# A selective scan whose output is projected in tiles of 16 steps by 8 samples instead of 128 steps of one sample

## What is computed

```python
def step(h, inputs):
    ad, bd, xt, ct = inputs
    h = jnp.clip(h * ad[:, :, None] + bd[:, :, None] * xt[:, None, :], -10.0, 10.0)
    yt = jnp.einsum('bd,bdh->bh', ct, h)
    return (h, yt)
...
y = ys.transpose(1, 0, 2) + D * xn
return y * jax.nn.silu(gate) @ W_out.T
```

## Time and profile before

| | us |
|---|---|
| median of 3 runs | 709.54 (709.09 to 712.57) |
| the profiled execution, its time | 711.52 |
| the same, its span (first to last instruction) | 709.7 |
| DVE busy | 500.8 (71%) |
| PE busy | 508.3 (72%) |
| ACT, POOL busy | 263.4, 130.1 |
| DMA | 64.88 MB, mean 91 GB/s |

### The profile page before, as it was taken

How to read it: one execution, slowest core, us unless ns; L and a number is a source line. 1 busy time by engine, 2 the same in 40 slices (tenths; PEclk the granted TensorE clock), 3 DMA queues, 4 the chain that set the end, 5 groups by cost and what they waited for, 6 DMA issues and landing times.

```text
span 709.7 us, 10868 instructions
## 1 busy us (share of the span) xinstructions
PE 508.3 (72%) x3248; PEld 301.2 (42%) x3264; DVE 500.8 (71%) x820; ACT 263.4 (37%) x513; POOL 130.1 (18%) x136
## 2 busy tenths in 40 slices
PE   3567888788888887999993000077777767898878
PEld 3455556465654644678883000011111112233367
DVE  2724759577585766556666898289999967999942
ACT  2314554535545342267663547011222212222211
POOL 5302012020210200060000235203131102223100
PEclk9858999999999998999996555579999989999999
DMA  9734161724427150021000134645545545556441
GB/s 356 229 67 100 36 118 21 132 44 89 96 38 133 31 102 0 1 115 63 0 0 1 49 116 157 105 77 103 98 95 99 106 86 106 132 124 143 85 149 52
DMA packets 44889, 64.88 MB, mean 91 GB/s; under 512 B 19536, under 2 KB 34256, under 8 KB 41152
## 3 DMA queue, kind: packets, MB, share of 16 engines
q1 hardware_dynamic: 41520, 59.26, 37.6%
q0 software_dynamic: 784, 3.15, 1.1%
q10 hardware_dynamic: 2560, 2.16, 0.9%
HBM read 41.88 MB, written 22.61 MB: 91 GB/s over the span
## 4 chain that ended last, share of the span: by engine, by line
PE 31%; DVE 23%; issue 21%; DMA 9%; ACT 7%; POOL 6%; SPq 2%; ACTq 0%; POOLq 0%; DVEq 0%
DVE zst L1377 19%; PE bank L718 6%; ACT ex L540 5%; PE bank L736 4%; DMA bst<-bd_d 3%; DMA qst<-mT 3%; PE bank L746 3%; PE bank L773 2%; PE bank L975 2%; PE bank L1061 2%; PE bank L965 2%; PE bank L727 2%; PE bank L756 2%; DVE mx L1175 2%; POOL xpart L416 2%
## 5 line engine op out<-in xcount | busy, mean ns | idle before, releaser
L1377 DVE CUSTOM_DVE_ANT_0 zst<-zst,bank,hi 128x512 f32<-128x512 f32 x256 | 191.5, 748 | 34.7 <-PE bank L965 26.1
L965 PE MATMUL bank<-xst,bst 128*128 128x512 bf16 x240 | 83.1, 399 | 98.6 <-DMA bst<-bd_d 60.2
L648 ACT ACTIVATE yb<-bank,ybias 128x512 f32<-128x512 f32 x64 | 44.0, 688 | 178.3 <-PE bank L975 157.9
L965 PEld LDWEIGHTS bank<-xst,bst 128*128 128x128 bf16 x256 | 24.6, 98 | 179.0 <-DVE zst L1377 109.4
L1175 DVE TENSOR_REDUCE mx<-bank 128x2 f32<-128x512 f32 x128 | 80.0, 686 | 18.2 <-PE bank L736 17.1
L540 ACT ACTIVATE ex<-bank 128x512 f32<-128x512 f32 x128 | 66.0, 608 | 41.2 <-PE bank L746 23.6
L975 PE MATMUL bank<-zst,cst 128*32 128x512 f32 x512 | 69.7, 617 | 0.7 <-DVE zst L1377 0.7
L1193 DVE TENSOR_TENSOR esum<-ex 128x1024 f32<-128x1024 f32 x32 | 39.1, 1223 | 43.0 <-ACT ex L540 43.0
L1237 DVE SCALAR_TENSOR_TENSOR acc<-xrp,wcv,acc 128x256 f32<-128x256 f32 x96 | 40.2, 481 | 29.3 <-ACT acc L580 28.7
L877 PE MATMUL bank<-xres,win 128*128 (+1 forms) x256 | 57.6, 382 | 1.2 <-ACT gateT L585 0.7
L389 POOL TENSOR_TENSOR qk<-qk,part 128x512 f32<-128x512 f32 x16 | 20.1, 1258 | 196.6 <-ACT part L502 196.6
(11 more groups left out here) (169 smaller groups left out, 712.9 us busy)
## 6 DMA issues: line engine op xcount, KB each, us to landing
qk_d<-part SPq DMA_DIRECT2D x64, 96.0 KB, 2.5
xs_d<-xpart SPq DMA_DIRECT2D x16, 384.0 KB, 2.6
xst<-xs_d SPq DMA_DIRECT2D x32, 192.0 KB
xst<-xs_d SPq DMA_DIRECT2D x32, 128.0 KB
y_d<-yb SPq DMA_DIRECT2D x128, 32.0 KB
ytk<-y_d SPq DMA_DIRECT2D x16, 256.0 KB, 3.7
bst<-bd_d SPq DMA_DIRECT2D x32, 102.0 KB
qst<-qk_d SPq DMA_DIRECT2D x8, 384.0 KB, 4.7
```

Source lines behind the costliest of these rows:

```text
L648: nc.scalar.activation(yb[:, par, g, :], bank[4 + n % 2][:, :], ACT.Identity, bias=ybias[:, bass.ds(i * (2 * CH // 4) + n, 1)]).then_inc(s ...
L965: mm(bank[k][:, :], bst[:, par, step, :], xst[:, par, step, :], start=True, stop=True)\
L1377: v._custom_dve(bass.dve_ops.TENSOR_ADD_SAT, out=zst[:, t % ZR, :], in0=zst[:, (t - 1) % ZR, :], in1=bank[t % 4][:, :], s0=hi[:, t:t + 1], ...
```

## The change

Rounds stay 16 steps (`RS`). What differs:

- An output tile is one round: 16 steps x 8 samples. The read-outs of all 16 steps accumulate in one bank (4 or 5 in turn): the weights of a step are laid in `cst` with shifted windows so that step 4g+k writes partitions 32k + 8g to 32k + 8g + 7, and zero elsewhere. `y_d` and the 128 + 16 DMAs of it are gone.
- ACT takes the bank with the bias to `ytk`, POOL adds D*xn from `dxk`, PE transposes, ACT copies and also makes the strided copy `x1s` (two instructions of 128 columns), POOL gates in four instructions of 128 columns, PE projects, ACT copies to `ob` (two buffers), SP stores with four DMAs. Tile r is done in round r+1, fifteen of them inside the scan; the last has DVE for the add and the gate.
- D*xn: POOL scales ten tiles before the first round and two in each of rounds 1 to 3. SP stores each to `dx_d` (eight DMAs of 256 KB before the loop, eight in round 3) and loads each round's 256 KB in `dxk` with four DMAs, two buffers.
- The scan inputs lie in two buffers of 16 steps instead of 8. The first round is loaded in halves (x: 8, 8, then 16 steps; b the same). A b load is two DMAs, rows 0 to 47 and 48 to 50.
- SP, POOL, ACT and PE have their rounds written out instead of loops.
- `ybias` comes from 16 small products instead of 4; POOL clears larger buffers at 301 us.

```diff
-            def load_x(par, ch):
+            def load_x(slot, first, count, name):
                 at = 0
                 for run in (3, 2, 1):
-                    sp.dma_start(xst[at:at + run * B, par, :, :],
-                                 xs_d[0:run, :, bass.ds(ch * CH, CH), :].rearrange("k b t c -> (k b) t c"))\
-                      .then_inc(s[f"ld_x{par}"], 16)
+                    sp.dma_start(xst[at:at + run * B, slot, first % RS:first % RS + count, :],
+                                 xs_d[0:run, :, first:first + count, :].rearrange("k b t c -> (k b) t c"))\
+                      .then_inc(s[name], 16)
                     at += run * B
-            def load_b(par, ch):
-                sp.dma_start(bst[0:KU, par, :, :], bd_v[:, bass.ds(ch * CH, CH), :]).then_inc(s[f"ld_b{par}"], 16)
+            def load_b(slot, first, count, name):
+                for lo, hi in ((0, KX), (KX, KU)):
+                    sp.dma_start(bst[lo:hi, slot, first % RS:first % RS + count, :],
+                                 bd_v[lo:hi, first:first + count, :]).then_inc(s[name], 16)
...
-            def store_chunk(par, ch):
-                for k in range(4):
-                    sp.dma_start(y_d[bass.ds(ch * CH, CH), :, :].rearrange("(g k) b c -> k b g c", k=4)[k],
-                                 yb[32 * k:32 * k + B, par, :, :]).then_inc(s[f"yst{par}"], 16)
+            def store_dx(half):
+                for b in range(B):
+                    sp.wait_ge(s["dx_ready"], half * B + b + 1)
+                    sp.dma_start(dx_d[half * P:(half + 1) * P, b, :], xc[:, b * HALVES + half, :]).then_inc(s[f"dx_out{half}"], 16)
+            def load_dx(r):
+                if r % (R // 2) == 0:
+                    sp.wait_ge(s[f"dx_out{r // (R // 2)}"], 16 * B)
+                if r >= 2:
+                    sp.wait_ge(s["ysum_ready"], r - 1)
+                for k in range(4):
+                    sp.dma_start(dxk[32 * k:32 * k + 32, r % 2, :], dx_by_tile[r, k])\
+                      .then_inc(s[f"ld_dx{r % 2}"], 16)
+            def store_out(r):
+                sp.wait_ge(s["ob_ready"], r + 1)
+                for k in range(4):
+                    sp.dma_start(out_by_tile[r, k], ob[32 * k:32 * k + 32, r % 2, :])\
+                      .then_inc(s[f"o_out{r % 2}"], 16)
...
-            load_x(0, 0)
-            load_x(1, 1)
+            load_x(0, 0, RS // 2, "ld_xf")
+            load_x(0, RS // 2, RS // 2, "ld_x0")
+            load_x(1, RS, RS, "ld_x1")
             sp.wait_ge(s["bd_out0"], 16 * (len(PAIRS) + 3))
-            load_b(0, 0)
-            load_b(1, 1)
+            load_b(0, 0, RS // 2, "ld_bf")
+            load_b(0, RS // 2, RS // 2, "ld_b0")
+            load_b(1, RS, RS, "ld_b1")
             store_b(1)
             sp.wait_ge(s["bd_out1"], 16 * (len(PAIRS) + 3))
+            store_dx(0)
+            sp.wait_ge(s["yb_done"], 1)
+            load_dx(0)
+            load_dx(1)
+            for i in range(R):
+                if i + 2 < R:
+                    sp.wait_ge(s["u_done"], (i + 1) * RS)
+                    load_x(i % 2, (i + 2) * RS, RS, f"ld_x{i % 2}")
+                    load_b(i % 2, (i + 2) * RS, RS, f"ld_b{i % 2}")
+                if i == 3:
+                    store_dx(1)
+                if i >= 1 and i + 1 < R:
+                    load_dx(i + 1)
+                if i >= 2:
+                    store_out(i - 2)
...
+            # POOL
+            fill_c(0)
+            fill_c(1)
             pool.wait_ge(s["rem0"], NT)
             pool.wait_ge(s["sq_done"], NT)
+            scale_dx(0, 0, B)
+            scale_dx(1, 0, 2)
+            for i in range(1, R):
+                r = i - 1
+                pool.wait_ge(s["y_taken"], r + 1)
+                pool.wait_ge(s[f"ld_dx{r % 2}"], 64 * (r // 2 + 1))
+                nc.gpsimd.tensor_tensor(ytk[:, r % 2, :], ytk[:, r % 2, :], dxk[:, r % 2, :], ALU.add)\
+                    .then_inc(s["ysum_ready"], 1)
+                if i + 1 < R:
+                    pool.wait_ge(s["y_done"], i * RG)
+                    fill_c(i + 1)
+                pool.wait_ge(s["yt_taken"], r + 1)
+                for c in range(CT):
+                    rows = yT[:, c, :].rearrange("p (k g b) -> p k g b", k=4, g=RG)
+                    ins = nc.gpsimd.tensor_tensor(rows, rows, gate_by_tile[:, r, c], ALU.mult)
+                ins.then_inc(s["yg_ready"], 1)
+                if i <= 3:
+                    scale_dx(1, 2 * i, 2 * i + 2)
...
+            # ACT
+            for i in range(1, R):
+                take_y(i - 1)
+                take_yt(i - 1)
+                take_out(i - 1)
+            take_x1(R - 1)
+            take_out(R - 1)
...
+            # PE
+            u_steps(0)
+            for i in range(R):
+                for g in range(RG):
+                    G = i * RG + g
+                    if G + 1 < R * RG:
+                        u_steps(G + 1)
+                    y_steps(i, g)
+                    if i >= 1:
+                        if g == 0:
+                            tile_transpose(i - 1)
+                        elif g >= 2:
+                            tile_out(i - 1, g - 2)
+            tile_transpose(R - 1)
+            tile_out(R - 1, 0)
+            tile_out(R - 1, 1)
```

More of the change, by code:

```diff
@@ L41 @@
 XS = 4
[L42 to L49 removed]
+RS = 16
+R = S // RS
+RG = RS // 4
+ZR = 8
+CW = 32 * (RS + 1)
 HEADS = [2 * (2 * r + par) + o for o in range(HT) for par in range(2) for r in range(4)]
@@ L374, in _ @@
+            store_out(R - 2)
+            store_out(R - 1)
+            for t in range(2):
+                sp.wait_ge(s[f"o_out{t}"], (R // 2) * 4 * 16)
         @block.gpsimd
@@ L685, in _, with take_y, take_yt @@
-            for t in range(2):
-                act.wait_ge(s[f"o_out{t}"], stored[t] * 16)
+            def take_y(r):
+                act.wait_ge(s["y_done"], (r + 1) * RG)
+                if r >= 2:
+                    act.wait_ge(s["yt_done"], r - 1)
+                nc.scalar.activation(ytk[:, r % 2, :], bank[4 + r % 2][:, :], ACT.Identity, bias=ybias[:, r:r + 1])\
+                    .then_inc(s["y_taken"], 1)
+            def take_yt(r):
+                act.wait_ge(s["yt_done"], r + 1)
+                if r >= 1:
+                    act.wait_ge(s["o_done"], r)
+                nc.scalar.activation(yT[:, :, :], bank[6][:, :].rearrange("p (c s) -> p c s", c=CT), ACT.Copy)\
+                    .then_inc(s["yt_taken"], 1)
+                take_x1(r)
@@ new lines, in take_x1, with take_out @@
+            def take_x1(r):
+                for k in range(HT):
+                    ins = nc.scalar.activation(x1s[:, k, :].rearrange("p (k g b) -> p k g b", k=4, g=RG),
+                                               x1_by_tile[:, r, k], ACT.Copy)
+                ins.then_inc(s["x1s_ready"], 1)
+            def take_out(r):
+                act.wait_ge(s["o_done"], r + 1)
+                if r >= 2:
+                    act.wait_ge(s[f"o_out{r % 2}"], (r // 2) * 4 * 16)
+                nc.scalar.activation(ob[:, r % 2, :], bank[7][:, 0:H], ACT.Copy).then_inc(s["ob_ready"], 1)
@@ L1400, in _ @@
-            gate(len(TAIL) - 1)
+                v._custom_dve(bass.dve_ops.TENSOR_ADD_SAT, out=zst[t % ZR], in0=zst[(t - 1) % ZR], in1=bank[t % 4][:, :],
+                              s0=hi[:, t:t + 1], s1=0.0).then_inc(s["z_ready"], 1)
+            r = R - 1
+            dve.wait_ge(s["y_done"], R * RG)
+            dve.wait_ge(s[f"ld_dx{r % 2}"], 64 * (r // 2 + 1))
+            v.scalar_tensor_tensor(ytk[:, r % 2, :], bank[4 + r % 2][:, :], ybias[:, r:r + 1], dxk[:, r % 2, :],
+                                   ALU.add, ALU.add).then_inc(s["ysum_ready"], 1)
```

320 lines of the change are left out of this document (79 added, 241 removed).

## The result

| | before | after |
|---|---|---|
| median of 4 runs, us | 709.32 (708.14 to 712.57) | 719.66 (714.16 to 721.83) |
| ratio after / before, 95% interval | | 1.0104 (1.007 to 1.0139) |
| profiled execution, its span | 711.52, 709.7 | 721.83, 720.0 |
| first scan step | 464.13 | 478.34 (+14.2; forecast +5.5) |
| first to end of last step | 210.7 | 229.9 (+19.2; forecast +1.0) |

The forecast was 692.0 with a range of 684 to 703: wrong in size and in sign. The last three rows make up the whole span, so they sum, but for rounding, to its +10.3. Of the +14.2 of the first step 0.7 lies ahead of the split of B (445.76 against 445.10).

The account below looks back on a forecast made before the run. VectorE's chain of dependent scan steps was taken as the bound. Tail -24.0, start +5.5 and scan +1.0, together -17.5, took the profiled 711.52 us to 694.0; the median lying 2.0 lower, the forecast was 692.0, range 684 to 703.

Parts of the forecast that it names:

- The tail: From the last scan step to the end: one tile left instead of nine, 10.8 us instead of 34.8, -24.0.
- Start (a): Before the scan: POOL's ten D*xn scalings hold VectorE's split of the B factor, +2.5 us, bounds 0 and +3.2.
- Start (b): Before the scan: 1536 KB of x instead of 768 ahead of the first b load, net +3 us, bounds 0 and +5.5.
- the credit of 1.6 for b in two parts: At the start: b loads cut into 48 and 3 rows should use all DMA engines, -1.6 us.
- The scan, 0.39 a round: In the scan: the projection's second half holds the next step in 14 rounds, 14 x 0.39 = 5.5 us.
- The new wait of 0.2 a round: In the scan: bias, add and transposes come later, so VectorE waits 0.2 us a round, 14 x 0.2 = 2.8.
- Rival 2: The tile chain holds the scan: hand-overs 2 us late would cost 28 us, giving 720; chance 0.10.
- D*xn at the start, +3 (bounds 0 and 8): Early scan: late D*xn and third x load hold steps 24 and 32, together 3 us, between 0 and 8.
- The steady round, "no wait": Steady scan rounds: a 16-step load takes 5.5 us plus some 2 to land, needed 15 us later: no wait.
- Rival 1: DMA sets the pace: D*xn and output loads and stores at 48 GB/s need the whole round, giving 703; chance 0.20.
- The old 10.6 us of waits that go: In the scan: the old kernel's ten waits, 10.6 us, go; the small ones are counted anew in other terms.

Follow-up runs that it names:

- e7: The changed kernel with POOL's first ten scalings held until VectorE has split the B factor; 714.07 us, ratio 1.0043 to the kernel before.
- e8: The kernel before with only each b load cut in rows 0 to 47 and 48 to 50; 706.68 us, ratio 0.9932.
- e2: The changed kernel with the first b load issued right behind the first x load, the other first loads after them; 718.86 us, ratio 1.0101.
- e6: e2 with the second half of B stored in round 1 instead of ahead of the D*xn stores; 711.25 us, ratio 1.0014 to the kernel before.
- e11: The changed kernel without D*xn: no scalings, stores or loads of it, zeros added instead; 691.53 us, ratio 0.9712 to the kernel before.
- e3: The changed kernel with dx_d laid out so both sides of D*xn loads and stores begin with 32 rows; 706.37 us, ratio 0.9926.
- e12: e11 with the first loads ordered as in e2, the second half of bpart stored in round 1 and four output buffers; 682.63 us, ratio 0.9593.
- e9: The changed kernel with the third x and b loads issued ahead of the first D*xn loads; 712.75 us, ratio 1.0019 to the kernel before.

## Why the prediction was wrong, step by step

**The tail** held: -23.0 for -24.0. From the copy to the end it is 1.3 longer, by SP's issue (0.616 instead of 0.4, the upper bound's 0.58) and the landing.

**Start (a)**, POOL beside the split: +2.95 for +2.5, inside its bounds. e7 shows cause and size.

**Start (b)**, the queue ahead of the first b: +10.6 for +3, outside my bound of 5.5. The step that failed is "while such a load ran, the DMA engines moved 176 GB/s": taken from a window of 2 us. The same window's row says share 0.87; the one to look for was the end of the same load. At the 89 GB/s of after's windows 768 KB more are 8.6 us (an estimate: other transfers share these windows), and the credit of 1.6 for b in two parts is not there (e8). e2 shows that the order alone can take the whole loss away; e6, with `store_b(1)` out of the way as well, starts no earlier (12.7 behind the split against 12.0).

**The scan, 0.39 a round**: right. **The new wait of 0.2 a round**: not there; ACT, POOL and PE meet their times in every undisturbed round, and e11 has none. Rival 2 as I described it (strided gates, late hand-overs) is not what happened, though its 720 is the time measured and its path, bias, add, transposes, u, is the one by which late stores reached DVE at 88 and 200. What I had not seen is what stands at the head of that path: ACT's wait for a free `ob`.

**D*xn at the start, +3 (bounds 0 and 8)**: the waits of steps 24, 32 and 36 are 13.1. Two sub-steps failed: D*xn was in dxk at 496.4 and not 487, as the stores were issued only at 482.43, behind 18.19 us of issues (the 8 us for 2 MB were right, 7.7, but I had no price for a blocked SP), and the third load took 14.84 us instead of 11. Part of the first is luck: the scan itself started 8.7 late, so that counted from the first step D*xn came at 18.1 where I had 17.4. The third load landed at 32.9 where I had 26.4, and it cost the most.

**The steady round, "no wait"**: 972 KB at 100 GB/s are 9.7 us and 384 KB at some 90 GB/s 4.3, together 14.0 if one after the other, in a round of 12.9 (16 x 0.783 + 0.39); both are estimates from the windows above. They overlap in part, so most rounds keep up; the one before step 200 does not, and the one before step 88 does not behind 2 MB of stores. My 5.5 + 2 for the load was the mis-sized term. Rival 1, that DMA sets the pace, named the right cause and read the four engines rightly: by the Trainium skill, "DMA: Bandwidth & Descriptors", section "Why a DMA increments its semaphore by 16 and not by 1", the count of engines is the largest up to 16 that divides the slowest dimension of both sides, so 4 rows against 32 use four. The trace agrees: the share is 0.25 in the window 595:599, and 0.47 with e3's 32 rows, though the GB/s there are nearly the same, 87 and 92, so this is not what the steady round lacks. But on it I put 48 GB/s (three engines' rate) where 87 were measured, and on the x loads 176 where 100 were: one error up, one down, and 703 instead of 720. It had a chance of 0.20.

**The old 10.6 us of waits that go**: gone in e11; in e8, half of them (10.6 to 5.3) go from the old kernel by one line.

**Not settled**: why a load of 48 long rows ends slowly (that its last rows lie on few engines is only argued); why the load behind e12's 4.20 takes 16.22 us; why SP is held at its issues; what the 16-step buffers would do in the old kernel; output stores in another shape; what part of e3's gain is the loads', the stores' or SP's issue time; how much of a wait varies from one execution to the next.

## What to carry to other kernels

Price a transfer by a whole transfer of its kind, from issue to landing, including the thin end, and never by its best window: here 100 GB/s against 176 stands behind the late start, the late third load and the steady round that slips. Where transfers crowd, try the shape before the schedule: the DMA share of a quiet stretch times 16 tells how many engines a shape uses (0.19 and 0.25 here, three and four), and one new layout (e3) brought more than any new order. List, for each engine that works in order, what it waits for ahead of the critical chain: an output store that nobody reads held the scan through ACT, and two more buffers gave 0.8%, and a transfer moved up in a saturated queue moves the wait (e2) or most of it (e9).
